# Adaptive-norm block with a selective scan and local attention: rounded-part products, early first loads and new written-out orders in its second phase

## The reference

```
h = layernorm(x) * (1 + ca) + sa
x = x + ga * scan_mixer(h)                    # 512 inner channels, 16 states, recurrence over 512 tokens
h = layernorm(x) * (1 + cb) + sb
x = x + gb * stack(h)                         # two layers of the following
# one layer, t = the residual stream:
q, k, v = split(shift_token(t) @ wqkv)        # 256 -> 3 * 512, 8 heads of 64
q, k = rotary(l2norm(q) * qs), rotary(l2norm(k) * ks)
o = softmax(q k^T in windows of 128, one window back) v
t = t + o @ wo                                # the projection: 512 -> 256
h = shift_token(t)
h = (h - mean(h)) / sqrt(var(h) + 1e-5) * lg + lb      # the mean and the variance
a, g = split(h @ w1 + b1)                     # 256 -> 2 * 682
t = t + (a * gelu(g)) @ w2 + b2
```

## Time and profile before

| | |
|---|---|
| time, median of 3 runs | 4311.34 us (4310.83 to 4312.2) |
| the profiled execution | 4316.54 us, its span 4314.5 us |
| PE / DVE / ACT / POOL busy over the span | 94% / 85% / 62% / 61% |
| scan phase | 0 to about 1795 us |
| second phase | about 1798 to 4314 us |
| mean granted TensorE clock | 0.981 |

### The profile page before, as it was taken

One profiled execution on the slowest core, in us unless ns is written; L12 is line 12 of the kernel. 1 busy time (PEld: TensorE's weight loads), 2 busy tenths in 40 slices (PEclk: granted clock), 3 DMA queues, 4 the chain that ended last, 5 costly groups with the idle time before them and its releaser, 6 DMA issues.

```text
span 4314.5 us, 60081 instructions
## 1 busy us (share of the span) xinstructions
PE 4052.9 (94%) x19614; PEld 2629.3 (61%) x19614; DVE 3679.9 (85%) x5981; ACT 2672.4 (62%) x5767; POOL 2639.3 (61%) x1297
## 2 busy tenths in 40 slices
PE   7999999999999999659999999999999999999997
PEld 4444444444444444347777777777777777777775
DVE  4999999999999999668888788888888888888873
ACT  5666666666666665335656565665656566565654
POOL 3999999999999999553434434343434334343432
PEclk8999999999999999879999999999999999999998
DMA  2333333333333333421000000001010100101000
GB/s 96 108 118 121 123 120 118 118 118 119 122 118 118 121 121 112 144 78 35 16 27 19 26 21 25 21 17 63 29 68 21 35 26 27 33 25 35 20 30 25
DMA packets 118499, 295.02 MB, mean 68 GB/s; under 512 B 21208, under 2 KB 43664, under 8 KB 118192
## 3 DMA queue, kind: packets, MB, share of 16 engines
q1 hardware_dynamic: 116320, 291.15, 20.2%
q10 hardware_dynamic: 1872, 0.05, 0.0%
HBM read 248.52 MB, written 42.64 MB: 67 GB/s over the span
## 4 chain that ended last, share of the span: by engine, by line
PE 34%; DVE 14%; issue 4%; ACT 4%; DMA 1%; SPq 0%; POOL 0%; DVEq 0%; ACTq 0%
PE b_bank L1407 12%; PE b_bank L1428 6%; PE b_bank L1296 5%; PE b_bank L1357 3%; PE b_bank L1373 3%; PE b_bank L1286 3%; ACT b_scores L1506 2%; DVE b_scores L1728 2%; DVE b_qk L1680 2%; DVE b_qk_rate L1669 2%; PE b_bank L1326 1%; PE b_bank L1346 1%; DVE b_qk_rot L1695 1%; DVE b_qk_rot L1701 1%; DVE b_xc L1785 1%
## 5 line engine op out<-in xcount | busy, mean ns | idle before, releaser
L813 POOL TENSOR_TENSOR a_state<-a_state,a_c_wide 128x1024 f32<-128x1024 f32 x512 | 1196.0, 2369 | 37.4 <-DVE a_state L755 37.4
L1628 POOL TENSOR_TENSOR b_scores<-b_scores,b_row_rate 128x1024 f32<-128x1024 f32 (+1 forms) x256 | 426.5, 1682 | 969.6 <-DVE b_row_rate L1745 969.6
L573 PE MATMUL a_y_sum<-a_state,a_ident 128*128 128x512 f32 x2048 | 942.3, 598 | 0.7 <-POOL a_state L813 0.6
L755 DVE TENSOR_TENSOR_SCAN a_state<-a_decay,a_slot 128x1024 f32<-128x1024 f32 x352 | 788.9, 2271 | 1.9 <-ACT a_decay L684 0.6
L1296 PE MATMUL b_bank<-b_w_qkv,b_hx_part 128*128 128x512 f32 x2304 | 661.7, 426 | 35.2 <-DVE b_w_qkv L1830 16.2
L1506 ACT ACTIVATE b_scores<-b_scores,b_row_bias 128x256 f32<-128x256 f32 (+1 forms) x1024 | 478.0, 469 | 269.9 <-DVE b_row_bias L1734 269.9
L573 PEld LDWEIGHTS a_y_sum<-a_state,a_ident 128*128 128x128 f32 x2048 | 387.1, 191 | 401.0 <-issue 342.4
L684 ACT ACTIVATE a_decay<-a_dt,a_neg_a 128x512 f32<-128x512 f32 x704 | 458.8, 711 | 164.0 <-DVE a_state L755 163.8
L1407 PE MATMUL b_bank<-b_hn_part,b_w 128*128 128x512 f32 x2112 | 515.4, 399 | 25.6 <-DVE b_hn_part L1652 25.6
L1296 PEld LDWEIGHTS b_bank<-b_w_qkv,b_hx_part 128*128 128x128 f32 x2304 | 424.0, 193 | 157.7 <-issue 48.2
L1601 POOL TENSOR_TENSOR b_by_cos<-b_qk,b_rotary 128x1024 f32<-128x1024 f32 x128 | 336.7, 2631 | 252.0 <-DVE b_qk L1680 249.9
...
## 6 DMA issues: line engine op xcount, KB each, us to landing
a_c_wide<-bc_rows SPq DMA_DIRECT2D x256, 512.0 KB, 3.7
...
```

The lines of the kernel that those rows point to most:

```text
L573: last = nc.tensor.matmul(y_sum[dd][:], ident[:], state[state_ring.slot[q]][:, i, :], start=False, stop=(j == GROUPS - 1 and i == GROUP - 1))
L755: nc.vector.tensor_tensor_scan(flat(h), flat(factor), flat(term), 0.0, ALU.mult, ALU.add).then_inc(scan_done.sem, 1)
L813: nc.gpsimd.tensor_tensor(h[:], h[:], c_wide[c_ring.slot[q // 2]][:], ALU.mult).then_inc(cmul_done.sem, 1)
L1628: nc.gpsimd.tensor_tensor(probs, probs, row_rate[:, w, at].unsqueeze(2).to_broadcast([P, 4, hi - lo]), ALU.mult)\
```

## The change

Five things change. (1) `wo`, `mean` and `var` are made from rounded parts: 12 products in place of 4 per half of `wo`, and 2 in place of 1 for `mean` and `var` (the matrix of 1/256 is exact when rounded). Attention's output is copied by ScalarE into an upper part, and VectorE makes the lower part where it had made the one copy; the operands of `mean` and `var` are cut by two more VectorE operations each; the weights `wo` are cut once per layer. (2) The squares use the memory of `qk`, so they wait for the products with cosines and sines, and those with sines wait for the transposes. (3) The first rows and weights of the second phase are loaded in the scan phase's last pass, ahead of its last x1 store, into memory that is free by then; the wait for the last stores moves behind the first loads of the second phase. (4) The scan phase gets one more slot each for decays, C and B. (5) Both lists are new, and the second phase's first pass has a list of its own, `FIRST_ORDER`. To make room, the rows for the projections, the parts of the normed rows and the residual rows share memory, which moves some loads' waits.

```diff
-DECAY_SLOTS, STATE_SLOTS, C_SLOTS, B_SLOTS = 3, 6, 2, 2
+DECAY_SLOTS, STATE_SLOTS, C_SLOTS, B_SLOTS = 4, 6, 3, 3
@@ store_x1 (SyncE, scan phase)
+                if isinstance(s, int) and s == BATCH - 1:
+                    for signal, per_pass in ((xs_full, INNER_CHUNKS), (z_full, INNER_CHUNKS), (bc_full, 1), (dt_full, INNER_CHUNKS)):
+                        wait(sp, signal, s, per_pass)
+                    wait(sp, h2_stored, 0, 1)
+                    first.load(sp)
                 wait(sp, x1_done, s, CHUNKS)
                 sp.dma_start(x1_dram[s], x1_t[:]).then_inc(x1_stored.sem, 16)
...
-            sp.wait_ge(x1_stored.sem, x1_stored.at(BATCH))
-            sp.wait_ge(h2_stored.sem, h2_stored.at(BATCH))
@@ ORDER, one line of each
-score:2.0 pt:1.0 cen:0 pn:1.0 mask:2.0 resload:0 pt:1.1 pn:1.1 store:0 sq:0 pt:1.2 pt:1.3 prot:0 psq:1 vc:1 pq:1 sqs:0
+FIRST_ORDER = """
+pss:0 pnorm:0 prot:0 padd:0 pq:0 pk:0 v:0 pss:1 psq:0 prate:0 vc:0 psq:1 prate:1 ptc:0 pnorm:1 pk:1 prot:1 vc:1 vc:2
@@ pipeline, second phase
-                for name, lead, *at in SCHEDULE:
+                for name, lead, *at in FIRST_PASS if i < 0 else SCHEDULE:
@@ load_hx, load_res (SyncE)
-                sp.wait_ge(v_done.sem, v_done.at(s))
+                if s < 3 or s == BATCH:
+                    sp.wait_ge(v_done.sem, v_done.at(s))
+                if s >= 3:
+                    sp.wait_ge(g_full.sem, g_full.at(s - 3, HID_CHUNKS))
...
+                if s > 0:
+                    sp.wait_ge(g_full.sem, g_full.at(s - 1, HID_CHUNKS))
                 wait_spare(sp, s, 4)
@@ project_out (TensorE)
-                product(s, f"wo{m}", w_o, m * P, [o_t[:, p, :] for p in range(PAIRS)])
+                parts = [(weights, x, p) for weights, x in ((w_o[0], upper), (w_o[1], upper), (w_o[0], lower)) for p in range(PAIRS)]
+                for n, (weights, x, p) in enumerate(parts):
+                    last = nc.tensor.matmul(psum.tile(f"wo{m}")[:].rearrange("p (a f) -> p a f", a=2),
+                                            weights[:, p, m * P:(m + 1) * P].bitcast(F32R), x[p].bitcast(F32R),
+                                            start=(n == 0), stop=(n == len(parts) - 1))
@@ mean, var (TensorE)
-                psum.filled(nc.tensor.matmul(psum.tile("mean")[:], mean_mat, x2_sum[:], start=True, stop=True), "mean")
+                averaged(s, "mean", sum_parts)
+            def averaged(s, name, parts):
+                for n, x in enumerate(parts):
+                    last = nc.tensor.matmul(psum.tile(name)[:], mean_mat[:].bitcast(F32R), x.bitcast(F32R), start=(n == 0), stop=(n == 1))
+                psum.filled(last, name)
@@ square_qk (ScalarE)
-                        act.wait_ge(qk_sum_done.sem, qk_sum_done.at(s, w))
+                        act.wait_ge(by_cos_done.sem, by_cos_done.at(s, w))
+                        act.wait_ge(by_sin_done.sem, by_sin_done.at(s, 2 * w))
@@ copy_out (ScalarE new, VectorE changed)
+                nc.scalar.activation(o_upper[:, :, w * WINDOW:(w + 1) * WINDOW].bitcast(F32R),
+                                     psum.tile(f"o{w}")[:].rearrange("p (n c) -> p n c", c=WINDOW), ACT.Copy).then_inc(o_upper_done.sem, 1)
-                nc.vector.tensor_copy(o_t[:, :, w * WINDOW:(w + 1) * WINDOW], psum.tile(f"o{w}")[:].rearrange("p (n c) -> p n c", c=WINDOW))\
+                nc.vector.tensor_tensor(o_lower[:, w // 2, :, at:at + WINDOW].bitcast(F32R),
+                                        psum.tile(f"o{w}")[:].rearrange("p (n c) -> p n c", c=WINDOW),
+                                        o_upper[:, :, w * WINDOW:(w + 1) * WINDOW], ALU.subtract).then_inc(o_t_done.sem, 1)
@@ add_residual, add_squares (VectorE)
+                    cut_sum(s, x2_sum[:], sum_parts, x2_added)
+                cut_sum(s, sq[:, 0, :], sq_parts, sq_added)
+            def cut_sum(s, x, parts, signal):
+                upper, lower = parts
+                dve.wait_ge(signal.sem, signal.at(s, 1))
+                nc.vector.tensor_copy(upper.bitcast(F32R), x).then_inc(signal.sem, 1)
+                dve.wait_ge(signal.sem, signal.at(s, 2))
+                nc.vector.tensor_tensor(lower.bitcast(F32R), x, upper, ALU.subtract).then_inc(signal.sem, 1)
@@ class FirstLoads
+    def load(self, sp):
+        for c in range(CHUNKS):
+            sp.dma_start(self.rows(c), self.stack_dram[0, :, c, :]).then_inc(self.hx_loaded, 16)
+        for i, done in enumerate(self.weights_loaded):
+            at = slice(i * INNER, (i + 1) * INNER)
+            sp.dma_start(self.weights[i][:], self.inp["L0_ffn_wqkv"][0].rearrange("(c p) f -> p c f", p=P)[:, :, at]).then_inc(done, 16)
```

More of the change, by code:

```diff
@@ L67, with __init__ @@
 class Banks:
-    def __init__(self, tiles, uses, count, since):
-        self.tiles, self.uses, self.count, self.since = tiles, uses, count, since
+    def __init__(self, tiles, uses, first, count, since):
+        self.tiles, self.uses, self.first, self.count, self.since = tiles, uses, first, count, since
         self.at = {use[0]: n for n, use in enumerate(uses)}
@@ L904, in stack_pass @@
         waiter = sb("waiter", [P, TILES * PAIRS])
-        hx = sb("hx", [P, CHUNKS, SEQ + 1])
+        hx, qkv_whole = first.hx, first.weights
+        hn_upper, hn_lower = (placed(f"hn_part{i}", [P, CHUNKS, SEQ], rows + 4 * (PAD + i * CHUNKS * SEQ)) for i in range(2))
+        x_res = placed("x_res", [P, CHUNKS, SEQ], rows + 4 * (PAD + CHUNKS * SEQ))
         hx_upper, hx_lower = (sb(f"hx_part{i}", [P, CHUNKS, SEQ]) for i in range(2))
@@ L1122, in blocks_of @@
+        uses = uses_of(SCHEDULE)
+        psum = Banks(banks_all, uses, uses_of(FIRST_PASS), SEQS, {f"y{i}": BATCH for i in range(2)})
         def blocks_of(w, i):
@@ L1189, in load_first @@
                         into += cols
+                for n in range(len(spare) - 1):
+                    load_spare(n)
                 load_w_o(0)
@@ L1282, in _ @@
         def _(pe):
-            def product(s, name, weights, cols, sources, rows=P):
-                psum.wait_free(pe, s, name)
-                for c, source in enumerate(sources):
-                    last = nc.tensor.matmul(psum.tile(name)[0:rows, :], weights[0:source.shape[0], c, cols:cols + rows], source,
-                                            start=(c == 0), stop=(c == len(sources) - 1))
-                psum.filled(last, name)
             def by_token(s, name, w, cols):
```

361 lines of the change are left out of this document (216 added, 145 removed).

## The result

The changed kernel takes 4180.99 us (median, 4179.33 to 4186.23) where the kernel before took 4311.77 us on the same chip; the ratio is 0.9697 with an interval of 0.968 to 0.9714. The prediction said 4227 us, range 4185 to 4270.

What follows compares the result with a forecast made beforehand. TensorE's own work was taken to bound the second phase, VectorE and GpSimd together the scan phase. 61 + 7.6 + 10 + 6 = 84.6 us off the profiled 4316.5, less 5.2 for the median, gave 4227 us, range 4185 to 4270.

Steps and rivals of the forecast that it cites:

- the scan phase: Scan phase: new order and slots take away some waits, 0.4 us a pass, 6 us (loss of 8 to gain of 25).
- VectorE and GpSimd hold each other: Scan phase: both engines are nearly full (719.6 and 714.0 of 740 us busy) and bound each other, with 3% to spare.
- The second phase: TensorE's projection, mean and variance in every pass: 1.9 us a pass shorter, times 32, 61 us (45 to 90).
- `wo` at 0.5 us a half: Second phase, output projection: twelve rounded products in place of four float32 save 0.5 us a half, two halves a pass.
- `mean` and `var` at 0.45 us each: Second phase: two rounded products in place of one float32 save 0.45 us on each, every pass.
- I add **nothing: Second phase, new order from `var` to `ga`: no gain or loss, bounds -0.5 to +1.0 us a pass.
- the tie ahead of `ga`: Second phase, `var` to `ga`: VectorE's 7.9 us against TensorE's 7.8, so TensorE still waits some 0.3 to 0.8 us.
- The boundary: Last scan-phase store to first projection: early loads cut 12.0 us to about 4.4, gain 7.6 us (4 to 9).
- The first pass: Second phase's first pass: squares no longer wait for the tile before, gain 10 us (3 to 17).
- Rival (b): Both phases: the lists also take waits away, another 20 us and 16 us, 4191 us; chance 0.18.
- Rival (c): Second phase: VectorE late at `ga`, held a microsecond by GpSimd in every pass, 31 us, 4258 us; chance 0.22.
- (d): Second phase: GpSimd's cosine product holds VectorE's sines 3.3 us every pass, 102 us, slower at 4329 us; chance 0.04.

Runs made afterwards that it cites:

- s1: The kernel before with the new list and new slots of the scan phase alone: 4271.28 us, ratio 0.9898.
- s5: The kernel before with two of TensorE's sums in the scan list each moved ahead of a spread of B that waits: 4288.19 us, ratio 0.9938.
- s6: The kernel before with one of TensorE's sums (unit 3) moved ahead of the variance in the scan list: 4315.75 us, ratio 1.0002.
- s7: The kernel before with three sums moved in the scan list, two ahead of spreads and one ahead of the variance: 4286.94 us, ratio 0.9938.
- m1: The changed kernel with the output projection `wo` in plain float32 again, copies and cuts kept: 4216.56 us, ratio 0.9771.
- m2: The changed kernel with mean and variance in plain float32 again, VectorE's cuts of their operands kept: 4201.02 us, ratio 0.9742.
- m3: The changed kernel with the second phase's first pass in the main list's order, not its own list's: 4188.6 us, ratio 0.971.

## Why the prediction was wrong, step by step

**The step that failed is the scan phase.** "I take 0.4 us a pass, 6 us (from a loss of 8 to a gain of 25)": it measured 44.4 us, and s1 shows that list and slots do it alone. The rows that give the size were on the table. VectorE was idle 740 - 719.6 = 20.4 us in 740, which is 2.9 us in a pass of 106, and its scans and products are the same before and after; a better order could give up to 16 x 2.9 = 47 us. I took as upper bound the two waits that the view names, 1.8 us a pass each, and priced them as overlapping and mostly kept. In fact VectorE's 1.8 us was a loss in full (s5: 26 us), GpSimd's was nothing (s6), and what the new list gains beyond s7 is in waits too short to stand out. "VectorE and GpSimd hold each other" was wrong as to GpSimd: it follows. The sum of the rest, 4227 + 6 - 44 = 4189 us, would have been in the range.

**The second phase: 61 us forecast, 62.8 measured, but not from the terms that I gave.** `wo` at 0.5 us a half: m1 shows 27 us by the centring and 32 by the ratios, against 32 forecast. Right. `mean` and `var` at 0.45 us each, 29 us: m2 shows 12 by the centring and 19 by the ratios. Two parts, which stand alone between other shapes, take 0.73 us, not 0.48 to 0.56. "I add **nothing**" for the rest of the list was wrong twice. In a plain pass the 2.61 us are 1.26 (m1) and 0.57 (m2), together 1.83 where 1.9 were forecast, and, if the two add up, 0.78 us of the new order, 24 us in 31 passes, which neither m1 nor m2 takes back. Most of it is idle time: TensorE's fell from 0.83 to 0.25 us, because the tie ahead of `ga` was broken in its favour (16.2 to 0.7 us). Against it stands what the order costs elsewhere: 31 x 2.61 = 81 us and 62.8 measured leave 18 us, of which 6.46 are the stop at the change of layer; the rest lies in the second layer's passes and the last two and wasn't taken apart. So 61 for 62.8 is luck as far as the list goes: two terms that were not in the sum, a gain and a loss, nearly cancelled.

By the Trainium skill (FP8 and Floating Point Precision, TensorE Precision Notes: true float32 is four passes) an estimate is that a half of `wo` in three rounded parts takes three quarters of float32, if a rounded product is one pass. m1 has 211.4 us for 58 halves in float32, 3.64 us, against 3.17: 0.87, so the trace does not bear the ratio out, and the step by the rows was the right one.

**The boundary** was right, 7.8 for 7.6 us, though its three terms add up to 4.1 us, not the 4.4 that were written (4.26 measured). **The first pass** too, 10.4 for 10 us; its squares stand 8.2 to 10.9 us apart, where 8 to 11 were forecast, but that their new memory does it was not shown by taking it back. What was behind the first mask, 4.4 us, had no term; m3 puts 1.2 us of it to the first list. Rival (b), the lists also take waits away, named the right mechanism in both phases, but its 16 us for the scan phase were too few. Rival (c), VectorE late at `ga`, did not come, nor did (d), the whole hold. The rows of the sines behind the first centring, before and after, show more than that:

```profile
L1695 DVE TENSOR_TENSOR b_qk_rot<-b_qk,b_rotary x240: 673/683/2905, 1966.6 to 4190.1; 128x512 f32<-128x512 f32 x120
L1773 DVE TENSOR_TENSOR b_qk_rot<-b_qk,b_rotary x240: 676/681/999, 1907.0 to 4064.7; 128x512 f32<-128x512 f32 x120
```

In the kernel before, one product with the sines in every pass took about 2.9 us (30 of the 240), in the passes looked at while GpSimd multiplied with the cosines (2145.62 to 2148.48, for one); the prediction took it for something that the change might bring. It was there already, and in the changed kernel it is gone: behind the first centring no product with the sines is over 999 ns. That is some 2 us a pass of room for VectorE, which was not priced; whether the new order or the squares' new memory did it wasn't tested.
